# Scale factors of the last four row tiles computed in two chains, the first of them on GpSimd

## What is computed

```python
def _layernorm(x, axis=-1, eps=1e-05):
    m = jnp.mean(x, axis=axis, keepdims=True)
    v = jnp.var(x, axis=axis, keepdims=True)
    return (x - m) / jnp.sqrt(v + eps)
...
        ts = t[0]
        support = x @ weight
        return (1.0 - ts) * support + ts * (adj @ support)
    x = _layernorm(x + _L0_gnn_ref(x, adj, L0_gnn_t, L0_gnn_weight), axis=-1)
```

## Time and profile before

| | before |
|---|---|
| median of 3 runs | 383.44 us |
| the profiled execution's own time | 383.85 us |
| its span, first to last instruction | 382.6 us |
| TensorE busy | 376.6 us (98%) |
| VectorE / ScalarE / GpSimd busy | 62% / 38% / 6% |
| granted TensorE clock | 0.999 of full speed |
| DMA | 84.4 MB, mean 221 GB/s |

### The profile page before, as it was taken

The page is one execution under the profiler, slowest core; times in us unless marked ns, Lnnn a source line. Parts: engine busy times, 40 slices in busy tenths (PEclk is TensorE's granted clock), DMA queues, the critical chain, the costliest instruction groups (busy, mean ns, idle before and its releaser), DMA issues.

```text
span 382.6 us, 4167 instructions
## 1 busy us (share of the span) xinstructions
PE 376.6 (98%) x1686; PEld 310.8 (81%) x1686; DVE 237.6 (62%) x335; ACT 145.7 (38%) x114; POOL 22.2 (6%) x19
## 2 busy tenths in 40 slices
PE   9999999999999999999999999999999999999994
PEld 5888888888888888888888888888888888888884
DVE  4978955447879466844577446873477643697305
ACT  4767544243352434324424325244332344423102
POOL 1202300003000010000100001000100001000000
PEclk9999999999999999999999999999999999999999
DMA  7999997555465766557665666756647567321001
GB/s 258 418 392 418 415 420 265 190 217 207 179 231 208 257 217 233 184 214 258 218 202 194 208 244 212 243 197 213 212 179 274 174 267 270 119 106 55 2 0 56
DMA packets 19107, 84.42 MB, mean 221 GB/s; under 512 B 1936, under 2 KB 6800, under 8 KB 11408
## 3 DMA queue, kind: packets, MB, share of 16 engines
q1 hardware_dynamic: 18656, 83.89, 59.7%
q10 hardware_dynamic: 432, 0.26, 0.2%
HBM read 79.95 MB, written 4.19 MB: 220 GB/s over the span
## 4 chain that ended last, share of the span: by engine, by line
PE 98%; DVE 1%; ACT 0%; issue 0%; DVEq 0%
PE agg L563 30%; PE agg L562 30%; PE agg L561 30%; PE out_ps L624 3%; PE out_ps L625 2%; PE out_ps L676 1%; PE agg L573 1%; PE agg L577 1%; PE agg L581 0%; ACT x_raw L325 0%; DVE x_raw L529 0%; DVE stats L533 0%; PE out_ps L645 0%; PE out_ps L647 0%; PE out_ps L646 0%
## 5 line engine op out<-in xcount | busy, mean ns | idle before, releaser
L359 DVE TENSOR_TENSOR a_lo<-a_raw,a_hi 128x2048 fp32r<-128x2048 f32 x60 | 137.4, 2291 | 111.1 <-ACT a_hi L263 111.1
L561 PE MATMUL agg<-a_hi,x_hi 128*128 128x512 f32 x504 | 196.3, 389 | 0.0
L563 PE MATMUL agg<-a_hi,x_lo 128*128 128x512 f32 x504 | 196.2, 389 | 0.0
L562 PE MATMUL agg<-a_lo,x_hi 128*128 128x512 f32 x504 | 196.1, 389 | 0.0
L263 ACT ACTIVATE a_hi<-a_raw 128x2048 fp32r<-128x2048 f32 x60 | 114.7, 1913 | 129.0 <-PE agg L563 123.7
L561 PEld LDWEIGHTS agg<-a_hi,x_hi 128*128 128x128 f32 x504 | 94.6, 188 | 19.8
L563 PEld LDWEIGHTS agg<-a_hi,x_lo 128*128 128x128 f32 x504 | 94.6, 188 | 19.8
L562 PEld LDWEIGHTS agg<-a_lo,x_hi 128*128 128x128 f32 x504 | 94.6, 188 | 19.6
L340 POOL TENSOR_TENSOR xt<-xt,omt_col 128x1024 f32<-128x1024 f32 x8 | 18.1, 2257 | 292.4 <-DMA xt<-in_xT 292.4
L624 PE MATMUL out_ps<-w_split,z_hi 128*128 128x512 f32 x56 | 20.0, 397 | 0.0
L274 ACT ACTIVATE std<-var_eps 128x4 f32<-128x4 f32 x7 | 1.4, 206 | 47.7 <-DVE var_eps L400 47.7
(11 more groups left out here) (76 smaller groups left out, 95.9 us busy)
## 6 DMA issues: line engine op xcount, KB each, us to landing
a_raw<-in_adjT SPq DMA_DIRECT2D x60, 1024.0 KB, 4.8
xt<-in_xT SPq DMA_DIRECT2D x8, 512.0 KB, 5.6
rows<-in_x SPq DMA_DIRECT2D x8, 512.0 KB, 5.7
out<-x_raw SPq DMA_DIRECT2D x7, 512.0 KB, 2.9
x_raw<-in_first_run SPq DMA_DIRECT2D x6, 512.0 KB, 11.9
a_raw<-in_first_run SPq DMA_DIRECT2D x8, 256.0 KB, 4.6
a_raw<-in_first_run SPq DMA_DIRECT2D x4, 512.0 KB, 7.3
x_raw<-in_first_run SPq DMA_DIRECT2D x4, 128.0 KB, 3.9
```

The costliest lines, as they stand in the source:

```text
L359: nc.vector.tensor_tensor(a_lo[:, slot], a_raw[:, slot], a_hi[:, slot].bitcast(f32), ALU.subtract).then_inc(a_lo_ready[slot], 1)
L561: nc.tensor.matmul(bank, x_hi[:, j, cols], a_hi[:, slot, b], start=first, stop=False)
L562: nc.tensor.matmul(bank, x_hi[:, j, cols], a_lo[:, slot, b], start=False, stop=False)
L563: return nc.tensor.matmul(bank, x_lo[:, j, cols], a_hi[:, slot, b], start=False, stop=last)
```

## The change

The scale factors of the last chunk are made in two chains. `early` is tiles 0 and 1, `late` tiles 2 and 3.

- **Early**, on GpSimd, as soon as the two squares are done: var + eps, that to the power -0.5 (a TENSOR_TENSOR with a buffer of two columns of -0.5), and the four instructions of a Newton step, each waiting for the one before by a semaphore. The last raises `early_rstd_ready`.
- **Late**, on ScalarE and VectorE, the old chain on two columns in place of four; the root no longer waits for the squares.
- ScalarE scales tiles 0 and 1 once `early_rstd_ready` is up, and then tile 3 (`rstd_ready`), and issues the store of tile 3 alone. VectorE scales tile 2 alone, from PSUM. SyncE stores tiles 0, 1 and 2, in this order.
- TensorE's `add_features(3)` moves from ahead of the second half's products to behind those of tile 2.
- GpSimd fills one more constant, `minus_half`, at the start.

```diff
--- before.py
+++ after.py
...
+        minus_half = sb("minus_half", [P, 2])
...
+        early, late = slice(0, 2), slice(2, TILES)
...
@@ -238,13 +245,16 @@
                     if n == min(NORM_AFTER[d] + RING, TURNS - 1):
                         store(d)
             c = CHUNKS - 1
-            for i in range(2):
-                sp.wait_ge(normed_ready, c * TILES + i + 1)
+            for i in (0, 1, 2):
+                if i < 2:
+                    sp.wait_ge(act_normed_ready, i + 1)
+                else:
+                    sp.wait_ge(normed_ready, c * TILES + 1)
                 sp.dma_start(out[c * WIDE + i * P:c * WIDE + (i + 1) * P], normed(c)[:, i]
                              ).then_inc(stored[c % 2], 16)
             sp.wait_ge(stored[0], 16 * (CHUNKS // 2))
-            sp.wait_ge(stored[1], 16 * (CHUNKS // 2 - 1 + 2))
-            sp.wait_ge(act_stored, 16 * 2)
+            sp.wait_ge(stored[1], 16 * (CHUNKS // 2 - 1 + 3))
+            sp.wait_ge(act_stored, 16)
 
         def scalar_engine(act):
             def x_high(p):
@@ -317,16 +327,17 @@
                 act.wait_ge(y_ready[i], c + 1)
                 nc.scalar.activation(normed(c)[:, i], y_tile(i), ACT.Square, scale=feats ** -0.5,
                                      accum_out=mean_var[:, i, 1:2]).then_inc(square_ready, 1)
-            act.wait_ge(square_ready, 2)
             act.wait_ge(mean_var_ready, c * TILES + 2)
-            nc.scalar.activation(std[:, :], mean_var[:, :, 1], ACT.Sqrt, bias=eps_col[:, :]).then_inc(std_ready, 1)
+            nc.scalar.activation(std[:, late], mean_var[:, late, 1], ACT.Sqrt, bias=eps_col[:, :]).then_inc(std_ready, 1)
+            act.wait_ge(early_rstd_ready, 1)
+            for i in (0, 1):
+                nc.scalar.activation(normed(c)[:, i], y_tile(i), ACT.Copy, scale=rstd[:, i:i + 1]
+                                     ).then_inc(act_normed_ready, 1)
             act.wait_ge(rstd_ready, c + 1)
-            for i in (2, 3):
-                nc.scalar.activation(normed(c)[:, i], out_ps[i][:, 0:feats], ACT.Copy, scale=rstd[:, i:i + 1]
-                                     ).then_inc(act_normed_ready, 1)
-            for i in (2, 3):
-                act.wait_ge(act_normed_ready, i - 1)
-                act.dma_start(out[c * WIDE + i * P:c * WIDE + (i + 1) * P], normed(c)[:, i]).then_inc(act_stored, 16)
+            nc.scalar.activation(normed(c)[:, 3], out_ps[3][:, 0:feats], ACT.Copy, scale=rstd[:, 3:4]
+                                 ).then_inc(act_normed_ready, 1)
+            act.wait_ge(act_normed_ready, 3)
+            act.dma_start(out[c * WIDE + 3 * P:c * WIDE + 4 * P], normed(c)[:, 3]).then_inc(act_stored, 16)
 
         def pool_engine(pool):
             def x_low(p):
@@ -344,6 +355,7 @@
             for p in range(EARLY):
                 x_low(p)
             nc.gpsimd.memset(eps_col[:, :], EPS).then_inc(eps_ready, 1)
+            nc.gpsimd.memset(minus_half[:, :], -0.5).then_inc(half_ready, 1)
             nc.gpsimd.memset(z[:, 0, 0:P], 1.0).then_inc(ones_ready, 1)
             pool.wait_ge(ones_ready, 1)
             nc.gpsimd.affine_select(ident[:, :], z[:, 0, 0:P], pattern=[[-1, P]], base=0, channel_multiplier=1,
@@ -351,6 +363,25 @@
             pool.wait_ge(omt_ready, 1)
             for c in range(CHUNKS):
                 scale_xt(c)
+            pool.wait_ge(square_ready, 2)
+            nc.gpsimd.tensor_scalar(var_eps[:, early], mean_var[:, early, 1], EPS, None, ALU.add
+                                    ).then_inc(early_var_ready, 1)
+            pool.wait_ge(half_ready, 1)
+            pool.wait_ge(early_var_ready, 1)
+            nc.gpsimd.tensor_tensor(rstd0[:, early], var_eps[:, early], minus_half[:, :], ALU.pow
+                                    ).then_inc(early_rstd0_ready, 1)
+            pool.wait_ge(early_rstd0_ready, 1)
+            nc.gpsimd.tensor_tensor(newton_s[:, early], rstd0[:, early], rstd0[:, early], ALU.mult
+                                    ).then_inc(early_s_ready, 1)
+            pool.wait_ge(early_s_ready, 1)
+            nc.gpsimd.tensor_tensor(newton_q[:, early], newton_s[:, early], var_eps[:, early], ALU.mult
+                                    ).then_inc(early_q_ready, 1)
+            pool.wait_ge(early_q_ready, 1)
+            nc.gpsimd.tensor_scalar(newton_c[:, early], newton_q[:, early], -0.5, 1.5, ALU.mult, ALU.add
+                                    ).then_inc(early_c_ready, 1)
+            pool.wait_ge(early_c_ready, 1)
+            nc.gpsimd.tensor_tensor(rstd[:, early], newton_c[:, early], rstd0[:, early], ALU.mult
+                                    ).then_inc(early_rstd_ready, 1)
 
         def vector_engine(dve):
             def a_low(n):
@@ -534,25 +565,23 @@
             for i in (2, 3):
                 dve.wait_ge(stats_ready, c * TILES + i - 1)
                 nc.vector.bn_aggr(mean_var[:, i], stats[:, i]).then_inc(mean_var_ready, 1)
-            dve.wait_ge(square_ready, 2)
             dve.wait_ge(mean_var_ready, c * TILES + 2)
-            nc.vector.tensor_scalar(var_eps[:, :], mean_var[:, :, 1], EPS, None, ALU.add).then_inc(var_eps_ready, 1)
+            nc.vector.tensor_scalar(var_eps[:, late], mean_var[:, late, 1], EPS, None, ALU.add).then_inc(var_eps_ready, 1)
             dve.wait_ge(var_eps_ready, c + 1)
-            nc.vector.reciprocal(inv_var[:, :], var_eps[:, :]).then_inc(inv_var_ready, 1)
+            nc.vector.reciprocal(inv_var[:, late], var_eps[:, late]).then_inc(inv_var_ready, 1)
             dve.wait_ge(inv_var_ready, 1)
             dve.wait_ge(std_ready, c + 1)
-            nc.vector.tensor_tensor(rstd0[:, :], inv_var[:, :], std[:, :], ALU.mult).then_inc(rstd0_ready, 1)
+            nc.vector.tensor_tensor(rstd0[:, late], inv_var[:, late], std[:, late], ALU.mult).then_inc(rstd0_ready, 1)
             dve.wait_ge(rstd0_ready, c + 1)
-            nc.vector.scalar_tensor_tensor(newton_q[:, :], std[:, :], -0.5, rstd0[:, :], ALU.mult, ALU.mult
+            nc.vector.scalar_tensor_tensor(newton_q[:, late], std[:, late], -0.5, rstd0[:, late], ALU.mult, ALU.mult
                                            ).then_inc(newton_q_ready, 1)
             dve.wait_ge(newton_q_ready, c + 1)
-            nc.vector.scalar_tensor_tensor(rstd[:, :], newton_q[:, :], 1.5, rstd0[:, :], ALU.add, ALU.mult
+            nc.vector.scalar_tensor_tensor(rstd[:, late], newton_q[:, late], 1.5, rstd0[:, late], ALU.add, ALU.mult
                                            ).then_inc(rstd_ready, 1)
             dve.wait_ge(rstd_ready, c + 1)
             dve.wait_ge(stored[c % 2], 16 * (c // 2))
-            for i in (0, 1):
-                nc.vector.tensor_scalar(normed(c)[:, i], y_tile(i), rstd[:, i:i + 1], None, ALU.mult
-                                        ).then_inc(normed_ready, 1)
+            nc.vector.tensor_scalar(normed(c)[:, 2], out_ps[2][:, 0:feats], rstd[:, 2:3], None, ALU.mult
+                                    ).then_inc(normed_ready, 1)
 
         def tensor_engine(pe):
             def products(c, slot, j, b, k, first, last):
@@ -658,8 +687,7 @@
                     first_half_times_weights(i)
                 pe.wait_ge(xc_hi_ready, 1)
                 pe.wait_ge(xc_lo_ready, 1)
-                for i in (2, 3):
-                    add_features(i)
+                add_features(2)
                 pe.wait_ge(z_hi_ready[1], c + 1)
                 pe.wait_ge(z_lo_ready[1], c + 1)
                 for i in (0, 1):
@@ -667,9 +695,11 @@
                     low_times_weights(i)
                 pe.wait_ge(z_hi_ready[1], c + 2)
                 pe.wait_ge(z_lo_ready[1], c + 2)
-                for i in (2, 3):
-                    high_times_weights(i)
-                    low_times_weights(i)
+                high_times_weights(2)
+                low_times_weights(2)
+                add_features(3)
+                high_times_weights(3)
+                low_times_weights(3)
 
             bf16 = mybir.dt.bfloat16
             for _ in range(WARM):
```

More of the change, by code:

```diff
@@ L134, in gnn_layernorm_kernel @@
         eps_ready, ones_ready, ident_ready = sem("eps_ready"), sem("ones_ready"), sem("ident_ready")
+        half_ready = sem("half_ready")
         act_normed_ready, square_ready = sem("act_normed_ready"), sem("square_ready")
@@ L139, in gnn_layernorm_kernel @@
         inv_var_ready = sem("inv_var_ready")
+        early_var_ready, early_rstd0_ready, early_rstd_ready = sem("early_var_ready"), sem("early_rstd0_ready"), sem("early_rstd_ready")
+        early_q_ready = sem("early_q_ready")
+        early_s_ready, early_c_ready = sem("early_s_ready"), sem("early_c_ready")
         act_stored = sem("act_stored")
```

## The result

The changed kernel takes **384.52 us** (median of 13 runs, 384.05 to 385.65) against 383.33 us for the kernel before in the same comparison (13 runs). The ratio is 1.0031, with a 95% interval of 1.0023 to 1.0039: it is slower by 1.2 us, 0.9 to 1.5. The forecast was 384.3 and slower by 0.86 us; the range was 382.7 to 385.8.

The account below looks back on a forecast made before the run. TensorE holds 98% of the chain, so only the tail of some 5 us can change. Early factors at 380.0 + 3.46 give an end of 383.46 against 382.6: 383.44 + 0.86 = 384.3 us, range 382.7 to 385.8.

Parts of the forecast that it names:

- The chain on GpSimd: Early factors: six steps of 0.25 us, five gaps of 0.07, 0.4 for the power, ready at 380.0 against 379.24 before.
- estimate of the fixed part: Fixed cost of a small GpSimd instruction: 0.18 us by the skill's cycle accounting, giving 383.9 us; the forecast took 0.25.
- the 0.11 a step: GpSimd step cost by start-to-start times of the constants, 0.04 + 0.07: factors ready at about 378.3, 382.7 us; not used.
- step on TensorE's order: End of TensorE's products: two products leave the place ahead of tiles 0 to 2, so squares end 0.23 us earlier, at 377.67.
- The tile 3 products end where they did: TensorE's last products: two instructions only pass from one side of tile 2 to the other, so the late chain gains nothing.
- The scaling: ScalarE scaling tile 0 before the first store: 0.40 us, by the square of a tile in SBUF.
- The flow of the stores: From the first store's issue to the end: 0.8 + 1.55 + 0.6 us, later stores 0.37 apart, no DMA gap.
- rival 1: GpSimd's early chain is short, factors ready at 378.64, 382.94 us, up to 383.9 with steps of 0.18; chance 0.25.
- rival 2: GpSimd's power is a long routine of 1.90 us: 385.8 us; chance 0.20 with what lies between it and the forecast.
- Rival 3: Stores spread over more time are acknowledged sooner, passing the ceiling by 0.1 to 0.2: 382.5 us; chance 0.07.
- ceiling of the gain: Most the change could bring, if the two late stores flow last: end at 381.9, 0.7 us or 0.18% less, 382.7 us.
- 0.8 until data flows: Stores at the end: 0.8 us from the first store's issue until its data flows.

Follow-up runs that it names:

- the run with one step: The changed kernel with GpSimd's early chain cut to var + eps alone, power and Newton step left out, tiles 0 and 1 wrongly scaled: 383.06 us.

## Why the prediction was right, point by point

| step in us, the first from z_lo's start | forecast | measured |
|---|---|---|
| squares end | 377.67 - 375.16 = 2.51 | 2.65 |
| from there to the early factors | 380.0 - 377.67 = 2.33 | 379.47 - 377.17 = 2.30 |
| from there to the first store's issue | 0.5 | 380.03 - 379.47 = 0.56 |
| from there to the end | 2.95 | 3.07 |
| against the tail before | +0.86 | +1.14 |

**The direction and its mechanism held.** The chain meant to be early came late, and tile 3 and the store of tile 2 stood behind it. Shortening it by 1.1 us took 1.08 off the tail, lengthening it by 0.77 (0.69 and a gap of 0.08) put 0.77 on, and reordering what stands behind it took 0.62 off.

**The chain on GpSimd was sized well in sum, less so in its parts.** The ordinary steps took 0.19 to 0.23 in place of 0.25; the power took 0.72 in place of 0.25 + 0.4; the gaps were 0.07 to 0.09 as taken, but 0.15 ahead of the power, which waits for two semaphores. (When the power is made twice, the first, with both waits, again starts 0.15 behind, and the second, with one, 0.08.) The way to GpSimd was 0.09 (0.08 taken), the way back 0.03 (0.08 taken). That 2.33 forecast and 2.30 measured lie so close is partly luck: the five steps came to 1.01 us in place of 1.25, and the power (0.07 over), the gaps (0.13 over) and the way (0.01 over) made up for it. By the Trainium skill (GPSIMD Engine Reference, "Elementwise — side-by-side cycle accounting") the estimate of the fixed part was 0.18 us; this trace, with steps of 0.19 to 0.23, agrees with it better than with my 0.25. The other page of the Trainium skill named in the prediction (Perfetto Trace Analysis, "GPSIMD Engine Instruction") wants start-to-start times in place of spans. From step to step these were 0.27 to 0.29, which is the span of 0.19 or 0.20 and a gap of 0.07 to 0.09; for a chain of dependent steps the spans were good enough, and the 0.11 a step that its rule gave on the constants' spacing was far too low.

**The step on TensorE's order failed**, and the prediction had named this as a mark of it: the squares were to end 0.23 us earlier, and ended 0.09 earlier. I had let tile 0's products start at 375.65, which is 0.08 behind the end of z_lo's first half; in the profile the wait costs more: the first product starts 375.10 - 374.52 = 0.58 after z_lo's start, not 0.49, and the second 0.19 behind it in place of 0.12. "The tile 3 products end where they did" was wrong by 0.16 us too. That cost nothing here, since the late side did not decide, but it would have been part of the price had the early chain been short.

**The scaling was mis-sized, and an error the other way hid half of it.** The 0.5 us to the first issue held 0.08 for the way back and 0.40 for the scaling. They measured 0.03 and 379.50 to 380.01, 0.51. I had taken the scaling from the row of the square; the square's scale is a fixed number and this one's a column of factors, and no run separates whether that makes the difference.

```profile
379.50 0.51 ACT L334 ACTIVATE x_raw<-x_raw,rstd 128x256 f32<-128x256 f32 x1 [1.48 <-POOL rstd L383]
379.92 0.49 ACT L334 ACTIVATE x_raw<-x_raw,rstd 128x256 f32<-128x256 f32 x1
```

**The flow of the stores was mis-sized by 0.12 us**: SyncE issues its three 0.40 and 0.47 us apart, slower than one flows (0.39), and I had taken 0.37. The first of these gaps is as much ScalarE's as the queue's: tile 1 is scaled at 379.92 + 0.49 = 380.41, and its store is issued at 380.43. The second is the queue's own, since tile 2 had long been ready: the issue before it took 0.42. Row by row the table's differences are 0.14 - 0.03 + 0.06 + 0.12 = 0.29, which with 0.86 gives 1.15. The largest of them is the step on TensorE's order.

**The rivals.** The short chain (rival 1) did not come to pass, and the run with one step shows that it could not have been told from no change either: -0.50 in the tail. The long power (rival 2) did not either: 0.72 and not 1.9 us, 0.53 above its neighbours. Rival 3 had the last store acknowledged sooner than 0.6 us after its data. In the slices shown above the data ends near 382.5, 0.6 us before the end of the span, as before, so this did not come to pass. From issue to landing a store took 1.8 us in the change (median), where before it took 1.9 at SyncE and 2.2 at ScalarE, but that time holds the flow as well, and fewer stores are in flight together.

The ceiling of the gain was a little too high by its own rows: it starts from the end of tile 3's scaling (379.75) where the rule "0.8 until data flows" starts from the issue (379.80), so 0.62 and not 0.7.

## What to carry to other kernels

To start part of a chain of dependent small steps earlier on another engine pays only if that engine's steps are short enough: compare the whole length with the head start. Here the head start was 378.26 - 377.90 = 0.36 us over the root, and GpSimd's chain was 2.30 us long against 0.98 on VectorE (from 378.26 to 379.24). That makes 2.30 - 0.36 - 0.98 = 0.96 us, and the first store was issued 1.01 later (5.51 against 4.50). And look at what is put behind the wait: ready work queued in order behind a late factor, on ScalarE and in SyncE's queue, was a quarter to a half of the loss. Work taken from ahead of a wait only helps as far as the engine does not then arrive at the wait too early.

## What the runs showed of the hardware that I had not expected

- A dependent step on two columns costs GpSimd 0.27 to 0.29 us from start to start and VectorE 0.20, on two columns and on four: less far apart than on a subtraction of 256 columns, which took 0.74 us on GpSimd and 0.42 on VectorE (z_lo). GpSimd's step took 0.20 both beside VectorE's scaling of tile 2 (L377 at 378.71) and after its end (L383 at 379.27), so the two engines did not slow each other here.
- The power of two columns took 0.72 us and 0.69 when it was made again, as much as a subtraction of 256 columns.
- A product behind a wait that is not yet over cost TensorE more than the input was late by: z_lo came 0.03 us after the weights of that product were due, the weights were loaded 0.15 late, and so was every product after it (the last one 2.20 us after z_lo's start in place of 2.04 before and 2.06 with the order undone), at a full granted clock (1.00).
- Issuing a store of 128 KB keeps ScalarE from its next scaling: with tile 3 first, the issue took 0.39 us, and the scaling of tile 0 began 0.04 behind its end, 0.19 after its factors.
- ScalarE's scaling of two tiles of 128x256 took 0.91 us from SBUF and 0.84 from PSUM.
